# A gated attention and FFN block: another order of the stages inside a batch, and another head

## What is computed

```python
xn = layernorm(x)
# attention without softmax: q, k, v are two-layer MLPs of xn with a Gelu between
q, k, v = (gelu(xn @ W1 + b1) @ W2 + b2 for each of q, k, v)
scores = tril(q @ k.T / sqrt(256 * 512))
s = layernorm(scores @ v) * ln_w + ln_b
# FFN, its weights quantised to -1, 0, 1 by the mean of their absolute values
h = relu(xn @ quantize(W1).T + b1)
g = silu(h @ quantize(W2).T + b2)
out = x + s * g
```

## Time and profile before

| | |
|---|---|
| time, median of 3 runs | 321.74 us (320.75 to 322.23) |
| the profiled execution's own time | 322.64 us |
| its span, first to last instruction | 320.8 us |
| busy: TensorE, VectorE, ScalarE, GpSimd | 96%, 75%, 72%, 40% of the span |
| mean granted TensorE clock | 0.983 of full speed |

### The profile page before, as it was taken

The page is one execution under the profiler, slowest core; times in us unless marked ns, Lnnn a source line. Parts: engine busy times, 40 slices in busy tenths (PEclk is TensorE's granted clock), DMA queues, the critical chain, the costliest instruction groups (busy, mean ns, idle before and its releaser), DMA issues.

```text
span 320.8 us, 5759 instructions
## 1 busy us (share of the span) xinstructions
PE 307.9 (96%) x1850; PEld 274.5 (86%) x1850; DVE 242.2 (75%) x556; ACT 230.1 (72%) x424; POOL 129.8 (40%) x106
## 2 busy tenths in 40 slices
PE   5998599999999999999999999999999999999993
PEld 5885499888998899888998899988998889988993
DVE  3589967797768887597787887597777977677677
ACT  1799553899549983799549984699648985599642
POOL 2015462526253542718245342817334362610223
PEclk9899599999999999999999999999999999999999
DMA  7943351320003100140003100050003200010001
GB/s 243 379 125 108 134 145 51 109 90 0 3 0 131 65 0 0 54 143 0 0 0 131 66 0 0 2 169 26 0 0 128 69 0 0 0 65 3 0 2 66
DMA packets 15771, 20.10 MB, mean 63 GB/s; under 512 B 1936, under 2 KB 12688, under 8 KB 15760
## 3 DMA queue, kind: packets, MB, share of 16 engines
q1 hardware_dynamic: 15056, 19.04, 17.7%
q10 hardware_dynamic: 704, 0.93, 0.8%
HBM read 15.74 MB, written 4.22 MB: 62 GB/s over the span
## 4 chain that ended last, share of the span: by engine, by line
PE 87%; DVE 5%; ACT 4%; DMA 2%; issue 1%; SPq 0%; DVEq 0%; ACTq 0%
PE bank L714 87%; DMA raw_qkv<-in_W2k 2%; ACT bank L367 1%; ACT g_hi L366 1%; DVE w2q L503 1%; DVE gw L584 1%; ACT r_lo L333 1%; DVE s L500 0%; DVE s_lo L614 0%; DVE x_stats L454 0%; ACT L366 0%; ACT o_square L340 0%; DVE s L604 0%; DVE x_all L639 0%; PE bank L699 0%
## 5 line engine op out<-in xcount | busy, mean ns | idle before, releaser
L557 DVE TENSOR_TENSOR r_lo<-bank,r_hi 128x512 fp32r<-128x512 f32 x64 | 42.5, 688 | 16.6 <-ACT bank L378 16.6
L377 ACT ACTIVATE r_hi<-bank,col 128x512 fp32r<-128x512 f32 x64 | 48.2, 754 | 0.0
L378 ACT ACTIVATE bank<-bank,col 128x512 f32<-128x512 f32 x64 | 46.9, 733 | 0.0
L296 POOL TENSOR_TENSOR y<-y,row 128x512 f32<-128x512 f32 x15 | 19.6, 1305 | 54.9 <-DVE gw L584 54.9
L714 PE MATMUL bank<-xT_lo,w1q 128*128 128x512 f32 x128 | 39.9, 393 | 0.1
L714 PE MATMUL bank<-xT_hi,w1q 128*128 128x512 f32 x128 | 39.8, 392 | 0.0
L280 POOL TENSOR_TENSOR y<-y,xn 128x512 f32<-128x512 f32 x14 | 23.6, 1683 | 37.3 <-DMA xn<-x_norm_rows 37.3
L289 POOL TENSOR_TENSOR v_lo<-v,v_hi 128x1024 fp32r<-128x1024 f32 x8 | 19.2, 2397 | 47.4 <-ACT v_hi L388 47.4
L392 ACT ACTIVATE y<-y 128x512 f32<-128x512 f32 (+1 forms) x17 | 10.3, 607 | 36.5 <-DVE y L575 36.5
L714 PE MATMUL bank<-w2q,r_lo 128*128 128x256 f32 x256 | 35.4, 281 | 0.0
L366 ACT ACTIVATE g_hi<-bank,col 128x512 fp32r<-128x512 f32 x48 | 33.2, 691 | 2.4 <-PE bank L714 2.3
(11 more groups left out here) (123 smaller groups left out, 703.9 us busy)
## 6 DMA issues: line engine op xcount, KB each, us to landing
out<-x_all SPq DMA_DIRECT2D x15, 256.0 KB, 2.6
x_all<-in_x SPq DMA_DIRECT2D x7, 512.0 KB, 3.6
y<-in_x_t SPq DMA_DIRECT2D x7, 512.0 KB, 3.4
xn<-x_norm_rows SPq DMA_DIRECT2D x7, 512.0 KB, 3.6
x_all<-in_w1t SPq DMA_DIRECT2D x1, 1024.0 KB, 8.1
x_all<-in_w2t SPq DMA_DIRECT2D x1, 1024.0 KB, 12.0
row<-in_rows ACTq DMA_DIRECT2D x1, 512.0 KB, 6.8
x_all<-in_x SPq DMA_DIRECT2D x1, 256.0 KB, 3.1
```

The lines of the kernel that those rows point to most:

```text
L296: nc.gpsimd.tensor_tensor(y[:, part], y[:, part], row[:, ROW_LNB:ROW_LNB + 1].broadcast_to((P, tiles, C)), ALU.mult).then_inc(gb_part, 1)
L377: nc.scalar.activation(r["hi"][:, f], pre[:], ACT.Relu, bias=b1)
L378: nc.scalar.activation(pre[:], pre[:], ACT.Relu, bias=b1).then_inc(f1_whole, 1)
L557: nc.vector.tensor_tensor(r["lo"][:, f], bank[(AT_F1 + f) % BANKS][:], r["hi"][:, f].bitcast(FP32), ALU.subtract).then_inc(r_split, 1)
```

## The change

The stages on TensorE come in another order: first layer (the k fills first, then q, then v: ORDER), keys, values, key sums, FFN one, scores, FFN two for tiles 0 and 1, FFN two for tile 2, weighted sums, FFN two for tile 3. In the last batch the weighted sums come ahead of tile 2. The other engines' orders follow:
- ScalarE: v_hi stands ahead of FFN one (in batch 0 behind its fourth fill); xT_hi of the next batch stands behind s_hi; the squares of tiles 0 and 1, silu of tiles 0 and 1, the squares of 2 and 3, silu of 2 and 3.
- VectorE: x_statistics of the next batch behind the second g_lo; z_lo, v32 and d ahead of the r_lo's; the first s_scale ahead of the last r_lo; xT_lo behind the s_lo's.
- The gate is last: gw = sum * rstd * ln_w (o_scale, VectorE), plus ln_b (GpSimd, offset), times silu (VectorE), plus x (VectorE, finish). weigh, the old gate and GpSimd's two offset ops on y and x go.
- SP: the load of x transposed stands behind the two stores; its wait for gb_made goes.
- Head: bias folds first, x of batch 0 in two halves, W2q in a buffer of its own with its bias as a 257th column (which replaces a part of the bias folds), the folds in two pieces, one inside the first layer; W1q is rounded and split by GpSimd; the Gelu table is loaded at the start; the sum of |W2| by VectorE; both thresholds together; W1 quantised in two halves of columns, W2 by VectorE (5 of 8 blocks, quantise2, amid the r_lo's) and GpSimd (3 of 8, quantise_rest); x of batch 1 loaded earlier.

The core of the diff:

```diff
-AT_L1, AT_F1, AT_K, AT_V, AT_D, AT_Y0, AT_S, AT_Y1, AT_O = 0, 6, 14, 16, 18, 19, 20, 24, 28
+AT_L1, AT_K, AT_V, AT_D, AT_F1, AT_S, AT_Y0, AT_Y1, AT_O, AT_Y2 = 0, 6, 8, 10, 11, 19, 23, 24, 25, 29
-AT_NONE = (26, 27)
+AT_NONE = (30, 31)
+ORDER = (2, 3, 0, 1, 4, 5)
...
 TensorE, batch:
+                for p, m in enumerate(ORDER):
+                    if first and p == 2:
+                        fold_weights(1)
...
+                for f in range(FT):
+                    if first and f == 0:
+                        pe.wait_ge(thr_made, 4)
+                    if first and f % (FT // 2) == 0:
+                        pe.wait_ge(w1_quantized, 2 * f // FT + 1)
+                    dst = claim(i, AT_F1 + f)
...
+                pe.wait_ge(r_split, 8 * i + 8)
+                if first:
+                    pe.wait_ge(w2_quantized, 1)
+                    pe.wait_ge(w2_rest_quantized, 1)
+                ffn_out(i, AT_Y0, (0, 1))
+                if last:
+                    weighted_sums()
+                ffn_out(i, AT_Y1, (2,))
+                if not last:
+                    weighted_sums()
+                ffn_out(i, AT_Y2, (3,))
...
 ScalarE, batch:
+                if not first:
+                    v_hi()
                 for f in range(FT):
...
+                    if first and f == 3:
+                        v_hi()
...
+                squares(0)
+                silu(0, 2, 3 * i + 1)
+                squares(1)
+                if not last:
+                    silu(2, 2, 3 * i + 3)
...
 VectorE, batch:
+                g_lo(1)
                 if not (first or last):
                     x_statistics(i + 1)
-                g_lo(0)
...
                 g_lo(2)
+                if first:
+                    dve.wait_ge(raw2_loaded, 16)
+                    nc.vector.tensor_reduce(abs_sum[:, 1:2], raw2.rearrange("p a b -> p (a b)"), mybir.AxisListType.X,
+                                            ALU.add, apply_absolute_value=True).then_inc(abs2_summed, 1)
                 g_lo(3)
                 g_lo(4)
                 g_lo(5)
...
+                for f in range(FT - 1):
+                    if first and f == 4:
+                        quantise2()
+                    r_lo(f)
...
                 s_scale(0)
+                r_lo(FT - 1)
                 for j in range(1, TT):
                     s_scale(j)
                     s_lo(j - 1)
...
+                def o_scale(h):
+                    dve.wait_ge(o_rstd_made, 2 * i + h + 1)
+                    for t in (2 * h, 2 * h + 1):
+                        nc.vector.scalar_tensor_tensor(gw[:, t], bank[(AT_O + t) % BANKS][:, 0:C], o_rstd[:, t:t + 1],
+                                                       row[:, ROW_LNW], ALU.mult, ALU.mult).then_inc(o_read, 1)
+                def finish(t, tiles, n):
+                    part = slice(t, t + tiles)
+                    dve.wait_ge(s_made, 2 * i + (1 if t == 0 else 2))
+                    dve.wait_ge(silu_made, 2 * i + n)
+                    nc.vector.tensor_tensor(gw[:, part], gw[:, part], y[:, part], ALU.mult).then_inc(s_gated, 1)
+                    dve.wait_ge(s_gated, 2 * i + n)
+                    nc.vector.tensor_tensor(x_all[:, i, part], x_all[:, i, part], gw[:, part],
+                                            ALU.add).then_inc(out_made, 1)
                 if not last:
+                    xT_lo(i + 1, [xT32[:, k] for k in range(CK)])
+                    dve.wait_ge(xT_split, 2 * i + 4)
+                    y_bias(AT_Y0, 0, 2, 3 * i + 1)
+                    y_bias(AT_Y1, 2, 1, 3 * i + 2)
+                    o_scale(0)
+                    y_bias(AT_Y2, 3, 1, 3 * i + 3)
+                    o_scale(1)
+                    finish(0, 2, 1)
+                    finish(2, 2, 2)
...
 GpSimd:
+                def offset(h):
+                    half = slice(2 * h, 2 * h + 2)
+                    pool.wait_ge(o_read, 4 * i + 2 * h + 2)
+                    nc.gpsimd.tensor_tensor(gw[:, half], gw[:, half], row[:, ROW_LNB:ROW_LNB + 1].broadcast_to((P, 2, C)),
+                                            ALU.add).then_inc(s_made, 1)
                 o_rstd_of(0)
+                offset(0)
                 o_rstd_of(1)
+                offset(1)
...
+            def quantise_rest():
+                rest = slice(FQ, FT)
+                pool.wait_ge(thr_made, 4)
+                nc.gpsimd.tensor_scalar(less, raw2[:, rest], neg_thr[:, 1:2], None, ALU.is_lt).then_inc(less_made, 1)
+                nc.gpsimd.tensor_scalar(w2q[:, rest], raw2[:, rest], thr[:, 1:2], None, ALU.is_gt).then_inc(more_made, 1)
...
 Head, TensorE:
-            fold_weights()
-            transpose_x0()
-            fold_biases()
+            fold_biases()
+            transpose_x0(range(TT))
+            fold_weights(0)
             batch(0, first=True)
```

More of the change, by code:

```diff
@@ L278, in xT_normalise @@
                 for k in range(CK):
+                    if after and k:
+                        pool.wait_ge(after, 1)
                     half = xT32[:, k].rearrange("q (t p) -> q t p", t=TT)
@@ L531, in batch @@
[L531 to L542 removed]
+                g_lo(2)
@@ L546, in batch @@
                 if first:
-                    x_statistics(1, second=True)
+                    thresholds(0)
+                    thresholds(1)
+                    dve.wait_ge(thr_made, 4)
+                    quantise1(0)
                 dve.wait_ge(e_made, i + 1)
@@ L594, in batch @@
                                                    ident[:], ALU.add, ALU.mult, accum_out=d[:, t:t + 1]).then_inc(d_read, 1)
-                if not last:
-                    dve.wait_ge(xT_split, 2 * i + 4)
-                y_bias(AT_Y0, 0, 2, 3 * i + 1)
                 dve.wait_ge(d_read, 4 * i + 4)
@@ L692, in claim, with transpose_x0 @@
                 return bank[at % BANKS]
-            def transpose_x0():
-                for t in range(TT):
+            def transpose_x0(tiles):
+                for t in tiles:
                     pe.wait_ge(xn_made, t + 1)
```

501 lines of the change are left out of this document (231 added, 270 removed).

## The result

The kernel with the change takes 338.25 us (median of 4 runs, 337.44 to 338.70), the kernel before 321.25 (median of 4, 320.33 to 322.23). The ratio is 1.0529, 95% interval 1.0495 to 1.0562: 17 us slower. The forecast was 336.9. The profiled execution took 337.44 us, with a span of 335.6, 14.8 us longer than that of before.

What follows compares the result with a forecast made beforehand. TensorE, busy 96% of the span, was taken as the bound, so middle batches could only gain waits. Head -0.8, batches +14.65 and end +1.3 gave +15.15 on 321.74, 336.9 us; own range 328 to 342, with rivals 325 to 346.

Steps and rivals of the forecast that it cites:

- V late by 1.45: Middle batches: the values stage starts 1.45 us late, waiting for VectorE's last g_lo; bounds 0.3 and 1.7.
- F: Middle batches: when VectorE finishes the old batch's work, counted from the batch's start, taken as 5.5 us.
- Y0 late by 0.85: FFN two for tiles 0 and 1 starts 0.85 us late, waiting for r_lo(7); bounds 0.65 and 1.0.
- The shared port: VectorE ops with two SBUF inputs and GpSimd ops reading SBUF exclude each other; values 1.45 late with it, 0.5 without.
- The head: Batch 0: batch 1 starts at 57.7 us instead of 58.5, -0.8; bounds -5.4 and +2.
- D waits 0.6 for a quantisation put ahead of e_lo: Batch 0: the key sums wait 0.6 us for a quantisation put ahead of e_lo.
- The end: Behind batch 7's last stage boundary: work ends at 4.25 us, not 2.97, +1.3; bounds 0 and +1.5.
- lower bound of the batches: Low end of the +14.65 us summed over the batches: +5.7, from 0.3 and 0.65.
- A: Rival: TensorE's clock falls once per middle batch, 1.7 us more each, 10 in all: 347 us; chance 0.12.
- B: Rival: values' wait covered, old batch's work finished by 4.1; only FFN two waits: 328.2 us; chance 0.14.
- C: Rival: both waits covered, r_lo(7) of batch 0 ready by 42, batch 1 5.4 earlier: 317.6 us; chance 0.11.
- D, no change: Rival: the waits replace each other, so the order does not move the time; chance 0.03.

Runs made afterwards that it cites:

- e45: The changed kernel with ScalarE's v_hi moved behind FFN one and VectorE's r_lo(7) ahead of the first score scaling; 332.75 us, ratio 1.0356.
- e3: The changed kernel with the next batch's x_statistics moved from behind the second g_lo to behind the sixth; 344.12 us, ratio 1.0686.
- e2: The changed kernel with GpSimd's two ln_b additions made on a buffer nobody reads, the gate not waiting for them; 336.75 us, ratio 1.0473.
- e6: The changed kernel with, in batch 0 alone, GpSimd's normalising of batch 1's x moved behind quantise_rest and v_lo; 334.65 us, ratio 1.0417.
- e7: The changed kernel with x_statistics behind v32, v_lo before GpSimd's root and normalising, r_lo(7) before the first score, batch 0's normalising behind quantising; 329.01 us.
- e8: The changed kernel with the old stage order put back on TensorE, ScalarE and VectorE, late gate and new head kept; 323.03 us, ratio 1.0046.
- e9: Old-order version of the changed kernel, with batch 0's thresholds and first w1q half earlier, v_shift sums behind Gelus, GpSimd's normalising behind quantising; 319.70 us, ratio 0.9935.
- e1: The changed kernel with GpSimd's two additions of ln_b per batch left out, the gate not waiting for them; 332.52 us, ratio 1.0346.

## Why the prediction was right, and where it was not

**Middle batches: the mechanism was right, both terms; one was too large.** Predicted were 1.45 + 0.85 = 2.3 us for each, 13.8 in all. Measured were 1.90 for each, 11.4 in all.
- *V late by 1.45: measured 1.11.* The chain holds link by link but for F. VectorE around the start of batch 3 (137.57), kernel after, the answers to the earlier trace rows:

```profile
138.11 0.87 DVE L674 SCALAR_TENSOR_TENSOR gw<-bank,o_rstd,row 128x256 f32<-128x256 f32 x2
139.73 1.56 DVE L691 TENSOR_TENSOR x_all<-x_all,gw 128x512 f32 x1
142.03 0.69 DVE L691 TENSOR_TENSOR x_all<-x_all,gw 128x512 f32 x1
147.31 2.48 DVE L578 TENSOR_TENSOR g_lo<-bank,g_hi 128x512 fp32r<-128x512 f32 x4
...
139.06 1.67 POOL L334 TENSOR_TENSOR gw<-gw,row 128x512 f32<-128x512 f32 x1 [1.04 <-DVE gw L674]
```

  The old batch's work ends at 142.72, so F = 5.15 and not 5.5: the scalings of tiles 2 and 3 ended 1.4 after the batch's start and not 1.7, since GpSimd's second root before them took 0.71 us and not 0.9, and began at -0.26 and not -0.1. From there to the end of the last g_lo at 149.79 are 7.07 us (predicted 7.09), and V starts 0.13 behind it, as predicted. The term that was mis-sized is this end of the old batch's work: its error, 0.35, times six batches is 2.1 of the 2.4 us by which the sum over the middle batches was too high.
- *Y0 late by 0.85: measured 0.71 by the starts,* and its first eight products then run 0.1 longer (1.21 against 1.11). With FFN one starting at 153.37, r_lo(7) ended 11.69 behind it (165.06) and not 11.85. v_hi in front of the Relus and the score in front of r_lo(7) are there as drawn (kernel after, ScalarE and VectorE):

```profile
153.82 1.06 ACT L415 CAST v_hi<-v 128x1024 fp32r<-128x1024 f32 x1 [4.12 <-DVE v L626]
163.35 0.77 ACT L426 ACTIVATE bank<-bank,col 128x512 f32<-128x512 f32 x1
...
163.59 0.34 DVE L641 SCALAR_TENSOR_TENSOR s<-bank,d,causal 128x128 f32<-128x128 f32 x1
164.38 0.68 DVE L656 TENSOR_TENSOR r_lo<-bank,r_hi 128x512 fp32r<-128x512 f32 x1
```

  e45 shows the two together as the cause: with both turned round, the wait is gone.
- *The two add up.* They do in after, and e45 takes one away and leaves the other; e3 shows the limit of it.

**The shared port.** That the offset's addition holds VectorE up was taken from one pair of rows, 1.10 against 0.68; here it is 1.56 against 0.69, in every batch, and e2 shows it with no dependence between the two. The Trainium skill (SBUF — State Buffer, "shared port pair") has it as a lock held for a whole instruction, and the traces agree: the addition ends 0.56 behind the end of GpSimd's (141.29 and 140.73, batch 3 of after), while the multiplication before it, which had begun first, kept its 0.68 and GpSimd's instruction took 1.67 and not 1.29. The prediction used it for the additions of the gate and for the quantising of W2, and not for what stands ahead of the key sums in the head.

**The head: the step that failed.** Predicted -0.8, measured +2.0. "D waits 0.6 for a quantisation put ahead of e_lo" took that quantisation at its length alone. GpSimd's normalising of batch 1 was not laid beside it: D waited 3.83, FFN one began at 31.28 and not near 29.5, the clock was at its lower level for its first four pairs (1.05 us instead of 0.63, until 34.6, which is 1.5 us), and the scores ended at 44.06 and not near 40.5. That TensorE then waited 3.87 us for r_lo(7), as the 3.8 predicted, is in part chance: both ends of the wait came 3.6 later than predicted, and in e6 the same wait is 5.46. From FFN two to batch 1 it took 12.6 and not 13.4, since the clock cost about 1.5 there and not the 2.3 carried over from the kernel before. e6 changes GpSimd's order only, and gives D's wait as 0.68, the scores' end at 39.4 where 40.5 was predicted, r_lo(7) at 44.84 where 44.3 was, and batch 1 at 57.39 where 57.7 was. The start of the first layer (10.15 against 10.2) and the wait for the last g_lo (0.76 against 1) were right.

**The end.** Predicted +1.3, measured +0.8. The last addition of 128x512 is held up as written down, kernel after:

```profile
329.91 1.63 DVE L691 TENSOR_TENSOR x_all<-x_all,gw 128x512 f32<-128x512 f32 x1
333.03 0.42 DVE L691 TENSOR_TENSOR x_all<-x_all,gw 128x256 f32<-128x256 f32 x1
...
329.35 1.64 POOL L334 TENSOR_TENSOR gw<-gw,row 128x512 f32<-128x512 f32 x1 [1.03 <-DVE gw L674]
```

This addition ended at 331.54, 1.86 behind the last stage's end at 329.68 and not 2.2, and the five instructions behind it took 1.91 us and not 2.05: together 0.5.

**The sum and the median.** The terms were +13.8 and +0.85, -0.8 and +1.3; measured were +11.4 and +0.6, +2.0 and +0.8. Errors of -2.7, +2.8 and -0.5 nearly cancel, and that is luck: the total of 14.8 is nearer to 15.15 than the terms are to theirs. In the lower bound of the batches, 5.7, the 0.65 of batch 7 is left out, so the lower end of the sum should have been 322.7 and not 322.0. The median moved by 17.0, 2.2 more than the profiled executions did; the profiled one of before was 1.4 above its median, and that of after 0.8 below.

**The rivals.** A, the clock falls as well: not in after. e3 shows that it can, at one wait of 1.85 us, and at a price of 1.6 us (the prediction had 1.7). B and C, the waits covered: F was 5.15, where 4.1 was needed, and r_lo(7) of batch 0 was ready at 47.88, where C needed 42. D, no change: the two waits did not replace each other in after; e3 is the kernel in which they do. What was costed at nothing was nothing: keys started 8.43 after the batch's start, TensorE waited for no xT and no bank, and the squares ran with Gelu's table and needed no load (the one load of that stretch, 1.28 us at 134.25, is silu's).

## What to carry to other kernels

Ask of a new order of stages not how busy the other engines are but what lies between each producer's last piece and its first use: here both waits arose with VectorE at 75% and ScalarE at 68%, and the old order of the same instructions has none. If work is to be moved out of a late chain, look at every other chain on that engine that it then stands in front of: in e3 the wait only moved. In e7, where it went behind the last link of both, the wait of the values was gone and the one before FFN two stayed small (0.33), though e7 changes three more things. And in each stretch that a change makes anew, lay GpSimd's instructions beside VectorE's before summing up durations.

## What the runs showed of the hardware that had not been expected

- **The clock fell after a wait of 1.85 us**, in four of six batches of e3 (mean 0.96, eight products in 1.91 us instead of 1.07), each time the same wait in the same place; in the others of the six it stayed at 1.00. Waits of 0.95 and 0.56 us in one batch, 15 us apart, left it at 1.00 in all six batches of after, and so did one of 2.60 in batch 0 of e2. What decides between the outcomes is open.
- **Instructions with one SBUF input are held up as well:** the comparison of 128x1024 against a threshold took 1.49 us beside GpSimd's normalising and 0.75 alone, and 2.02 beside it in e8. Beside another GpSimd instruction in e9 it took only 0.97 and ended first. Instructions with an input in a bank, as z_lo, were not (two in 1.40 in after and in e6 alike).
- **GpSimd pays too:** its addition of 128x512 took 1.67 us beside VectorE and 1.29 apart from it, at 136.00 in after; v_lo took 2.98 in batch 0 of after, with a median of 2.41 over its eight.
- **The first layer of batch 0 does not start at the same time in all kernels with the same head:** 10.15 in after, 11.77 in e8 and e9. The matmuls ahead of it took up to twice as long there (the four of the first weight fold 1.92 us and not 1.03, the transposes 1.95 and not 1.13, the first pair of the layer 1.42 and not 0.73), much as at the lower clock level (1.05 against 0.63 for a pair in batch 0 of after); in e1, where the first pair took 1.42 as well, the view gives 0.51 from 10 to 12 us. For e8 and e9 it gives 1.00 there, so that the clock is the cause is likely but not shown.
